# Attention scores in single 512-column steps, and a layer norm applied from bf16 copies

## What is computed

```python
def attn(x, Wqkv, bqkv, Wr, br):
    xh = x.reshape(b, c, h, he).transpose(0, 2, 1, 3)
    q, k, v = jnp.split(jnp.einsum('bhce,ef->bhcf', xh, Wqkv) + bqkv, 3, axis=-1)
    att = jnp.einsum('bhqe,bhke->bhqk', q, k) / jnp.sqrt(jnp.float32(he))
    mask = jnp.tril(jnp.ones((c, c), dtype=att.dtype), k=-1)
    att = jax.nn.softmax(att * mask, axis=-1)      # masked scores are 0, not -inf
    out = jnp.einsum('bhqk,bhke->bhqe', att, v)
    return out.transpose(0, 2, 1, 3).reshape(b, c, d) @ Wr + br
x = x + attn(_layernorm(x), ...)
x = x + ffn(_layernorm(x), ...)                    # router, shared expert, 8 experts
```

## Time and profile before

| | |
|---|---|
| median of 3 runs | 4044.59 us (4043.55 to 4231.99) |
| the profiled execution | 4052.05 us |
| its span, slowest core (core 3) | 4050.5 us (all cores 4039.2 to 4050.5) |
| busy share of the span | PE 73%, DVE 29%, ACT 20%, POOL 1% |
| granted TensorE clock, mean | 0.78 to 0.782 on all cores |
| chain that ended last | PE 70%, DVE 10%, ACT 9%, issue 8% |

### The profile page before, as it was taken

How to read it: one execution, slowest core, us unless ns; L and a number is a source line. 1 busy time by engine, 2 the same in 40 slices (tenths; PEclk the granted TensorE clock), 3 DMA queues, 4 the chain that set the end, 5 groups by cost and what they waited for, 6 DMA issues and landing times.

```text
span 4050.5 us, 45350 instructions; the slowest of 8 cores (4039.2 to 4050.5 us)
## 1 busy us (share of the span) xinstructions
PE 2950.1 (73%) x15380; PEld 1342.5 (33%) x15380; DVE 1168.2 (29%) x2386; ACT 817.2 (20%) x1034; POOL 28.8 (1%) x55
## 2 busy tenths in 40 slices
PE   2344444444444444483899999999999999999997
PEld 0122222222222222231344444444444444444443
DVE  5222222222222222236113333333333332333332
ACT  0122222222222222200221112121221112122110
POOL 0000000000000000000000000000000000000000
PEclk7555555555555555586899999999999999999998
DMA  2100000000000000004004040222204031221302
GB/s 85 32 1 1 1 1 1 1 1 1 1 1 1 1 1 1 1 9 76 1 11 73 1 84 1 42 42 43 42 1 84 1 63 22 42 42 27 58 1 83
DMA packets 7082, 98.77 MB, mean 24 GB/s; under 512 B 1860, under 2 KB 2260, under 8 KB 2260
## 3 DMA queue, kind: packets, MB, share of 16 engines
q0 software_dynamic: 3984, 77.81, 11.0%
q1 hardware_dynamic: 2884, 18.06, 1.3%
HBM read 165.10 MB, written 8.39 MB: 43 GB/s over the span
## 4 chain that ended last, share of the span: by engine, by line
PE 70%; DVE 10%; ACT 9%; issue 8%; DMA 1%; DVEq 1%; ACTq 0%; SPq 0%; POOL 0%
PE PM L769 25%; PE PM L858 25%; PE PS L464 6%; ACT PT L407 5%; PE PS L399 5%; ACT PT L448 3%; DVE SMASK L439 3%; DVE AVN L481 2%; PE PTR L488 2%; PE PS L336 2%; PE PS L531 1%; PE PS L431 1%; DVE RZ L476 1%; PE PS L353 1%; PE PS L362 1%
## 5 line engine op out<-in xcount | busy, mean ns | idle before, releaser
L769 PE MATMUL PM<-XLN,W 128*128 128x512 bf16 x4608 | 1028.3, 387 | 0.7 <-DVE WSB L727 0.7
L858 PE MATMUL PM<-H1G,W 128*128 128x512 bf16 x4608 | 999.6, 379 | 0.0
L786 ACT ACTIVATE H1G<-PM,B1C 128x512 bf16<-128x512 f32 x576 | 395.7, 687 | 1619.4 <-PE PM L769 1619.4
L769 PEld LDWEIGHTS PM<-XLN,W 128*128 128x128 bf16 x4608 | 456.8, 99 | 568.6 <-issue 58.1
L858 PEld LDWEIGHTS PM<-H1G,W 128*128 128x128 bf16 x4608 | 451.1, 98 | 544.2 <-issue 2.3
L835 DVE TENSOR_TENSOR H1G<-H1G,WB 128x512 bf16<-128x512 bf16 x512 | 217.9, 426 | 693.0 <-ACT H1G L786 693.0
L873 DVE TENSOR_TENSOR XRES<-XRES,PM 128x512 f32<-128x512 f32 x288 | 198.0, 687 | 652.9 <-PE PM L858 652.9
L407 ACT ACTIVATE PT<-PS 128x1024 bf16<-128x1024 f32 x192 | 196.4, 1023 | 718.7 <-PE PS L399 718.7
L464 PE MATMUL PS<-VA,PT 128*128 128x65 bf16 x2560 | 175.7, 242 | 214.6 <-ACT PT L448 214.6
L399 PE MATMUL PS<-QT,KT 64*128 64x512 bf16 x384 | 193.9, 606 | 185.6 <-ACT PT L407 185.3
L439 DVE TENSOR_TENSOR SMASK<-PS,MASKS 128x512 f32<-128x512 f32 x256 | 164.9, 686 | 543.2 <-PE PS L431 462.1
(11 more groups left out here) (99 smaller groups left out, 959.3 us busy)
## 6 DMA issues: line engine op xcount, KB each, us to landing
W<-w1cat POOLq DMA_DIRECT2D x9, 4096.0 KB, 28.1
W<-w2cat POOLq DMA_DIRECT2D x9, 4096.0 KB, 27.3
XRES<-xt SPq DMA_DIRECT2D x8, 1024.0 KB
ot<-XRES SPq DMA_DIRECT2D x8, 1024.0 KB
WRF<-wr_rl POOLq DMA_DIRECT2D x1, 2048.0 KB, 18.9
MASKS<-c_masks SPq DMA_DIRECT2D x1, 1024.0 KB
B1C<-b1col POOLq DMA_DIRECT2D x9, 8.0 KB, 27.3
B2C<-b2col_t POOLq DMA_DIRECT2D x9, 4.0 KB, 3.5
```

The source lines that it names most:

```text
L769: lambda e, psv=psv, kc=kc, ht=ht, tt=tt: e.matmul(psv, W1[:, kc * DFF + ht * 128: kc * DFF + (ht + 1) * 128], xln(kc)[:, tt * 512:(tt + 1 ...
L786: lambda e, h1sl=h1sl, psv=psv, e_i=e_i, ht=ht: e.activation(h1sl, psv, AF.Gelu, bias=B1C[:, (e_i % 2) * 16 + ht: (e_i % 2) * 16 + ht + 1]),
L858: lambda e, psv=psv, kc=kc, dtl=dtl, buf=buf: e.matmul(psv, W2[:, kc * D + dtl * 128: kc * D + (dtl + 1) * 128], H1G[:, buf * 8192 + kc * 512:
```

## The change

Layer norm. PB1 and PB2 are first copied from PSUM into SBUF as bf16, PB1 into XSQ (which is free by then) and PB2 into a new tensor B2SB; the first copy waits for all eight broadcast matmuls. Then per chunk there are one multiplication and one subtraction over all 2048 tokens. The f32 tensor TMP is gone. `emit_ln` returns one count per chunk: the projections of head h wait for chunk h // 2, and the router's matmuls over the first 512 tokens each wait for their own chunk.

Attention. The two loops over pairs become one over single key chunks, with one exponential of 512 columns for each. `sc_hist` gets one entry per unmasked key chunk and none from masked ones. The mask multiplication alternates between the halves of SMASK and waits for the exponential just before it, as earlier.

```diff
-                TMP = LE(nc.sbuf_tensor("TMPLN" + sfx, [128, 1024], F32))
+                B2SB = LE(nc.sbuf_tensor("B2SB" + sfx, [128, T], BF16))
...
+                    cb1 = P.emit("vector",
+                            lambda e: e.tensor_copy(XSQ[:], PB1[:]),
+                            waits=[("ST", tb[3])], inc="SV")
+                    cb2 = P.emit("vector",
+                            lambda e: e.tensor_copy(B2SB[:], PB2[:]),
+                            waits=[("SV", cb1)], inc="SV")
+                    applied = []
+                    prev = cb2
                     for c in range(NCH):
...
+                        va = P.emit("vector",
+                                    lambda e, c=c: e.tensor_mul(
+                                        xln(c), xres(c), XSQ[:]),
+                                    waits=[("SV", prev)], inc="SV")
+                        prev = P.emit("vector",
+                                    lambda e, c=c: e.tensor_sub(
+                                        xln(c), xln(c), B2SB[:]),
+                                    waits=[("SV", va)], inc="SV")
+                        applied.append(prev)
...
                     for j in range(NTT):
-                        if rot % 2:
+                        for kc in range(4 * j + 4):
+                            slot = rot % 6
                             rot += 1
...
+                            w = [slot_free[slot]]
+                            if len(sc_hist) >= 2:
+                                w.append(sc_hist[-2])
...
+                            if kc < 4 * j:
+                                ss_exp_last = P.emit("scalar",
+                                        lambda e, pts=pts, psv=psv: e.activation(
+                                            pts, psv, AF.Exp, scale=0.125),
+                                        waits=[("ST", ts)] + ptguard, inc="SS")
+                                slot_free[slot] = ("SS", ss_exp_last)
+                                sc_hist.append(("SS", ss_exp_last))
+                            else:
                                 d = kc - 4 * j
+                                smsl = SMASK[:, (kc % 2) * 512:(kc % 2) * 512 + 512]
                                 vm = P.emit("vector",
+                                        lambda e, smsl=smsl, psv=psv, d=d: e.tensor_mul(
+                                            smsl, psv, MASKS[:, d * 512:(d + 1) * 512]),
                                         waits=[("ST", ts), ("SQ", sq_masks),
                                                ("SS", ss_exp_last)], inc="SV")
+                                ss_exp_last = P.emit("scalar",
+                                        lambda e, pts=pts, smsl=smsl: e.activation(
+                                            pts, smsl, AF.Exp, scale=0.125),
+                                        waits=[("SV", vm)] + ptguard, inc="SS")
+                                slot_free[slot] = ("SV", vm)
...
                             if kc == 0:
-                                w = [("GQ", gq_rww), ("SV", ln2_done), pr_free]
+                                w = [("GQ", gq_rww), ("SV", ln2_applied[kc]), pr_free]
+                            elif tt == 0:
+                                w = [("SV", ln2_applied[kc])]
```

More of the change, by code:

```diff
@@ L381, in build_program @@
                     for j in range(NTT):
-                        if rot % 2:
+                        for kc in range(4 * j + 4):
+                            slot = rot % 6
                             rot += 1
[L384 to L406, removed]
-                                    lambda e, base=base, boff=boff, kc0=kc0: e.activation(
-                                        PT[:, kc0 * 512:(kc0 + 2) * 512],
-                                        base[:, boff:boff + 1024],
-                                        AF.Exp, scale=0.125),
-                                    waits=[("ST", ts)] + ptguard, inc="SS")
-                            slot_free[slot] = ("SS", ss_exp_last)
-                            slot_free[slot + 1] = ("SS", ss_exp_last)
-                            sc_hist.append(("SS", ss_exp_last))
-                            sc_hist.append(("SS", ss_exp_last))
@@ L416, in build_program @@
-                        for kc0 in range(4 * j, 4 * j + 4, 2):
-                            slot = rot % 6
-                            rot += 2
-                            base = (PS4 if slot < 4 else PS2)
-                            boff = (slot if slot < 4 else slot - 4) * 512
-                            vm = 0
-                            for q in range(2):
-                                kc = kc0 + q
-                                psv = base[:, boff + q * 512: boff + (q + 1) * 512]
-                                w = [slot_free[slot + q]]
-                                if len(sc_hist) >= 2:
-                                    w.append(sc_hist[-2])
-                                if kc == 0 and j == 0:
-                                    w += [("SS", ev_q[-1]), ("SS", ev_k[-1])]
-                                ts = P.emit("tensor",
+                            psv = (PS4[:, slot * 512:(slot + 1) * 512] if slot < 4
+                                   else PS2[:, (slot - 4) * 512:(slot - 3) * 512])
@@ L431, in build_program @@
+                            w = [slot_free[slot]]
+                            if len(sc_hist) >= 2:
+                                w.append(sc_hist[-2])
+                            if kc == 0 and j == 0:
+                                w += [("SS", ev_q[-1]), ("SS", ev_k[-1])]
+                            ts = P.emit("tensor",
                                         lambda e, psv=psv, kc=kc, j=j: e.matmul(
@@ L577, in build_program @@
                                 inc="B2S_", inc_n=16)]
-                ln2_done = emit_ln([[] for _ in range(NCH)])
+                ln2_applied = emit_ln([[] for _ in range(NCH)])
+                ln2_done = ln2_applied[-1]
                 _ckpt("ln2")
```

33 lines of the change are left out of this document (6 added, 27 removed).

## The result

The changed kernel takes 3934.93 us (median of 10 runs, 3928.2 to 4204.84) where the kernel before takes 4064.42 in its 10. The ratio is 0.9718, with a 95% interval from 0.9675 to 0.9762: faster. The profiled execution has a span of 3937.2 us on its slowest core (cores 3921.9 to 3937.2), 113 us less than the 4050.5 before.

What follows compares the result with a forecast made beforehand. The prediction took attention to be bound by a chain of waits, PE and ACT taking turns, and the experts by PE. Attention 105, layer norms 13 and router 2 us make 120 less: 4044.6 to 3924 us, range 3872 to 3962.

Steps and rivals of the forecast that it cites:

- What bounds the kernel: Whole kernel: experts bound by PE and untouched (2101.8 us); attention (1610.6 us) set by PE and ACT taking turns.
- Price of the exponential: Attention: a 512-column exponential takes 0.597 us from PSUM and 0.63 us from SMASK, by ACT's slope of 0.832 ns a column.
- The rival with 0.68 and 0.72: Attention: smaller exponentials cost as much as the evacuations, 0.68 and 0.72 us; 40 us more, 3964 us; chance 12%.
- Unmasked chunks: Attention: one exponential runs under the next matmul, two chunks take 1.43 us instead of 2.27; saves 8.6 us a head.
- The rival that the turns stay: Attention: PE and ACT still alternate, each unmasked chunk pays a full round trip of 1.43 us; 4175 us; chance 3%.
- Masked chunks: Attention: DVE and ACT alternate strictly, four steps of 1.50 us a block; loses 2.0 us a head.
- Attention in sum: Attention, 16 heads: unmasked gain of 8.6 less masked loss of 2.0 us a head, 105 us less.
- Layer norm and router: Ends of both layer norms: 6.6 us saved each, 13.2 in all; router logits earlier, 2 of 3 us counted.
- the double rate: Layer norm: rival that the mixed f32 and bf16 multiplication runs at double rate; 17 us less, 3907 us; chance 8%.
- Clock: Attention: rival that denser score matmuls lift TensorE's clock from 0.54 towards 1.00; 50 us less, 3874 us; chance 12%.

Runs made afterwards that it cites:

- deep: Changed kernel with the score matmul's wait for the exponential two back removed, leaving only its PSUM slot wait; rerun median 3846.9 us, ratio 0.9508.
- turns: Changed kernel with each unmasked exponential entered twice in sc_hist, so a score matmul waits for the one just before; median 4285.8 us, least disturbed pair 4198.
- pairs_deep: Kernel before with each unmasked pair's exponential entered once in sc_hist instead of twice, still 1024 columns and old layer norm; median 3870.3 us, ratio 0.9505.
- mask_pairs: Changed kernel with masked chunks in pairs again, one exponential of 1024 columns each; median 3975.4 us, least disturbed pair 3863.
- mask_free: Changed kernel where a mask multiplication waits only for the exponential that last read its own half of SMASK; median 3792.3 us, ratio 0.9138.
- attn_only: Kernel before with only the change's new attention loop over key chunks; median 4050.7 us, least disturbed pair 3939.
- ln_only: Kernel before with only the change's layer norm and router edits; median 4170.9 us; the same kernel run again (_b) 4033.2 us, ratio 0.9991.
- tail: Changed kernel with unmasked chunks paired, four-part SMASK, waits only for own slot or part, and block end regrouped (one reciprocal, four scalings together); 3500.4 us, ratio 0.8652.

## Why the prediction was right

Forecast were 3924 us (3872 to 3962) and faster by over 2%; measured were 3934.9 as the median, 3928 as the lowest run and 3925 on the least disturbed pair.

**What bounds the kernel.** It held: the experts didn't move, attention is a chain of turns, and making its turns overlap shortened it although the engines' work hardly shrank: PE went from 775.6 to 767.0 us busy, DVE grew from 346.8 to 358.9 and ACT from 406.7 to 446.8.

**Price of the exponential.** 0.597 and 0.63 us from the slope of two rows; measured 0.597 and 0.631. The rival with 0.68 and 0.72 is out. The evacuation of the same width that it was taken from differs in its bias operand, its function and its 64 partitions; which of them makes it dearer, no run tells.

**Unmasked chunks.** Round trip and period held: 1.43 us for two chunks forecast, 1.42 measured; unmasked parts of 3.28, 6.14 and 9.00 forecast, 3.25, 6.12 and 8.93 measured. Block j=3 became 4.1 us shorter, about 4 forecast. That it is the round trip and neither ACT nor PE, `deep` showed (0.49 us a chunk once the wait is gone), and that it is the depth and not the size, `turns` and `pairs_deep`. The rival that the turns stay is out, but its price was right: `turns` is that case, at 1.42 us a chunk. It took 4198 us where the rival's sum gave 4175; most of the difference is the start of the masked part, 0.97 us after the last unmasked exponential in `turns`, where that sum had 0.46 (0.5 us in 48 blocks, 24 us).

**Masked chunks.** The mechanism held and the size was a little low. Forecast were 1.50 us a step and 5.9 us a block, measured are 1.52 and 6.0: a step is 0.691 for the multiplication, 0.631 for the exponential, 0.09 from DVE to ACT and 0.10 back, where the forecast had 0.69, 0.63 and twice 0.09, and rounded down. The start behind the last unmasked exponential came 0.44 to 0.48 us after it, forecast 0.46. The loss is 1.0 us for j=0 and 0.5 for each other block, 2.5 us a head instead of 2.0. `mask_pairs` and `mask_free` showed that this alternation is what is paid for.

**Attention in sum.** By the first three rows of the table of distances 6.3 us a head (50.0 to 43.7), 100 us in all, forecast 105; 98 in the windows of the two profiled executions, 103 between the least disturbed pairs of the kernel before and `attn_only`.

**Layer norm and router.** The multiplication at 2.29 us was right, the double rate is out. The Trainium skill (VectorE: DVE Perf Modes, What auto-detection actually checks), which gives the double rate only where every tensor is 16-bit, agrees with the 2292 ns of the mixed operation and the 1226 ns of the one with bf16 alone. From the first copy to the end 34.5 us were forecast (70.13 to 104.6) and measured. One layer norm saves 6.3 to 6.5 us (6.6 forecast). The router's first logits come 3.0 us earlier, and none of it is lost where the forecast gave 1 us away: the transposes followed the logits at the old distance (1786.72 - 1785.44 = 1.28 us to the first copy, as 1899.47 - 1898.19 before), so the load of IDF didn't hold them up. `ln_only` and `ln_only_b` show the two together: 14 us between the least disturbed pairs, which the whole runs of `ln_only_b` don't tell from nothing.

**Clock.** It stayed (0.54 to 0.53 in attention). In `deep` and `tail` far denser score streams did not raise it either.

Between the least disturbed pairs the change is worth 117 us where 120 were forecast. The masked part's 0.5 us a head (8 us) is more than that difference, and the unmasked parts (0.1 us a head) and the router give some back; that the misses cancel in part is luck. The rest of the 11 us between forecast and median is the spread of the runs, whose lowest is 3928.

## What to carry to other kernels

When two engines take turns and neither is busy, count how far back each wait reaches before changing sizes. A list that records one operation twice halves the depth, and here one line was worth 200 us. Cutting operations in half pays only if something comes to overlap, since each piece pays the handovers again (with 512 columns 1.42 us a chunk at depth one, 0.71 at two, 0.49 when only the slot is waited for; with pairs 1.135 at depth one and 0.57 at two). A wait on the last user of a buffer should name the part that is overwritten; waiting for the last user of any part cost 2.4 us in each of 64 blocks of the changed kernel.

## What the runs showed of the hardware

The clock of TensorE stayed at 0.50 (1.2 GHz) under score matmuls back to back. In `tail`, block j=3 of head 1 sends 16 of them, each with 64 rows and 512 columns (timeline of PE, then windows of that stretch and of all of attention):

```profile
241.57 7.03 PE L399 MATMUL PS<-QT,KT 64*128 64x512 bf16 x16
```

```profile
241.60:248.60 7.00, 7.00 (x17) 1.81 (x16) 1.29 (x3) 5.84 (x7) 0.00 (x0) 0.50 0.00 0
122.50:1206.60 1084.10, 725.08 (x5633) 399.17 (x5634) 301.00 (x848) 409.83 (x576) 0.00 (x0) 0.55 0.00 1
```

16 matmuls in 7.03 us, PE busy throughout, and the granted clock is 0.50, as in the projections; the 128-row output projection of the same kernel has 1.00 from 1214 to 1218 us. The Trainium skill (TensorE: Matmul & The Clock Gate, What's actually happening) would have the half clock released by such sustained activity; here it was not.

Over all of attention the mean is 0.53 to 0.55 and not 0.50, because the clock does rise in it, in head 1 for one, though not in the scores. The windows just before that stretch:

```profile
236.00:238.00 2.00, 1.84 (x34) 1.68 (x31) 0.06 (x1) 0.00 (x0) 0.00 (x0) 0.57 0.00 0
238.00:240.00 2.00, 0.36 (x2) 0.21 (x2) 1.21 (x6) 0.00 (x0) 0.00 (x0) 1.00 0.00 0
```

It rises at the end of the 64 matmuls with V, which have 128 rows, and is at 1.00 while PE mostly waits for DVE; by the score matmuls it has fallen back to 0.50. In the kernel before, head 1 shows the same behind three of its four blocks (1.00 from 252 to 254 us, for one). So full clock came behind matmuls with 128 rows, and not in the stretches with 64 rows in which PE was busy throughout. That fits the number of rows as the reason, but the two also differ in columns, and no run separates them.

Handovers between engines were the same in every kernel that has the wait: 0.14 to 0.15 us from an exponential's end to the score matmul that waits for it, 0.10 from a score matmul's end to the exponential (0.15 for the first one of a block), 0.09 from a mask multiplication to the exponential and 0.10 from an exponential to the multiplication. With them and the durations of single operations, the stretches of the seven kernels that change attention's waits came out within 0.3 us of what was worked out, most of them within 0.15.
